# Gated cross attention on one core: how the column maxima reach all partitions, and where the gate work stands

## The reference

```
memory_proj    = memory @ W_mem.T
scores         = x @ memory_proj.T / sqrt(512)
attn           = softmax(scores)              # over the 1601 memory rows
memory_context = attn @ memory_proj
gate           = sigmoid([x, memory_context] @ W_gate.T + b_gate)
fused          = x + gate * memory_context
out            = fused * rsqrt(mean(fused**2) + 1e-6) * norm_w
```

## Time and profile before

| | us |
|---|---|
| median of three runs | 546.85 (546.77 to 548.07) |
| the profiled execution's own time | 546.85 |
| its span, first to last instruction | 544.8 |
| PE busy | 536.1 |
| DVE busy | 479.8 |
| ACT busy | 316.3 |
| POOL busy | 148.5 |

### The profile page before, as it was taken

The page is one execution under the profiler, slowest core; times in us unless marked ns, Lnnn a source line. Parts: engine busy times, 40 slices in busy tenths (PEclk is TensorE's granted clock), DMA queues, the critical chain, the costliest instruction groups (busy, mean ns, idle before and its releaser), DMA issues.

```text
span 544.8 us, 8828 instructions
## 1 busy us (share of the span) xinstructions
PE 536.1 (98%) x2432; PEld 438.8 (81%) x2432; DVE 479.8 (88%) x758; ACT 316.3 (58%) x601; POOL 148.5 (27%) x127
## 2 busy tenths in 40 slices
PE   8999999999999999999999999999999999999994
PEld 7877888888888888888888888888888888888883
DVE  3789959999799997899888997999979999789966
ACT  4676636565474755566365664666546575557523
POOL 0005600154002630046200650015400263004704
PEclk9999999999999999999999999999999999999999
DMA  9964372620575108831277114762068510301033
GB/s 227 270 130 78 93 119 67 108 72 27 137 163 113 59 0 170 176 87 39 79 132 160 62 39 111 158 106 84 12 144 165 113 49 15 120 26 40 1 117 116
DMA packets 184337, 54.25 MB, mean 100 GB/s; under 512 B 161528, under 2 KB 174848, under 8 KB 184320
## 3 DMA queue, kind: packets, MB, share of 16 engines
q1 hardware_dynamic: 183792, 53.52, 42.8%
q10 hardware_dynamic: 528, 0.52, 0.3%
HBM read 45.63 MB, written 8.39 MB: 99 GB/s over the span
## 4 chain that ended last, share of the span: by engine, by line
PE 96%; DMA 1%; DVE 1%; ACT 0%; SPq 0%; issue 0%; POOL 0%; POOLq 0%; ACTq 0%; DVEq 0%
PE bank L364 22%; PE bank L366 22%; PE bank L365 22%; PE bank L548 9%; PE bank L549 9%; PE bank L550 9%; PE bank L569 1%; PE bank L466 1%; DMA mem_raw<-in_ctx_dram 1%; PE bank L583 1%; PE bank L451 1%; PE bank L439 1%; DVE fused L1031 0%; DVE fused L1023 0%; SPq L312 0%; ACT squares_out L738 0%
## 5 line engine op out<-in xcount | busy, mean ns | idle before, releaser
L1185 POOL TENSOR_TENSOR psum_rows<-psum_rows,p_tmp 128x512 f32<-128x512 f32 (+1 forms) x88 | 123.0, 1398 | 71.6 <-ACT p_tmp L711 70.0
L875 DVE TENSOR_TENSOR p_lo<-p_tmp,p_hi 128x512 fp32r<-128x512 f32 (+1 forms) x104 | 92.6, 891 | 5.5 <-ACT p_hi L673 5.4
L1185 POOL TENSOR_TENSOR psum_rows<-p_tmp 128x512 f32<-128x512 f32 x8 | 10.4, 1300 | 276.2 <-ACT p_tmp L711 276.2
L711 ACT ACTIVATE p_tmp<-s 128x512 f32<-128x512 f32 (+1 forms) x104 | 64.5, 626 | 30.5 <-DVE s L916 29.3
L364 PE MATMUL bank<-q_hi,mt_hi 128*128 128x512 f32 (+1 forms) x208 | 81.8, 393 | 0.0
L365 PE MATMUL bank<-q_lo,mt_hi 128*128 128x512 f32 (+1 forms) x208 | 81.2, 390 | 0.0
L366 PE MATMUL bank<-q_hi,mt_lo 128*128 128x512 f32 (+1 forms) x208 | 81.2, 390 | 0.0
L548 PE MATMUL bank<-p_hi,mem_hi 128*128 128x512 f32 (+1 forms) x208 | 81.1, 390 | 0.0
L549 PE MATMUL bank<-p_lo,mem_hi 128*128 128x512 f32 (+1 forms) x208 | 81.0, 390 | 0.0
L550 PE MATMUL bank<-p_hi,mem_lo 128*128 128x512 f32 (+1 forms) x208 | 81.0, 389 | 0.0
L673 ACT ACTIVATE s<-bank 128x512 f32<-128x512 f32 (+1 forms) x104 | 62.0, 596 | 19.3 <-PE bank L366 18.9
(11 more groups left out here) (94 smaller groups left out, 1023.7 us busy)
## 6 DMA issues: line engine op xcount, KB each, us to landing
mem_raw<-in_ctx_dram SPq DMA_DIRECT2D x48, 256.0 KB, 3.0
mem_blocks<-in_ctx_dram SPq DMA_DIRECT2D x64, 136.0 KB
x_again<-in_x_dram SPq DMA_DIRECT2D x32, 256.0 KB, 2.7
out_dram<-fused SPq DMA_DIRECT2D x32, 256.0 KB, 2.1
x_raw<-in_x_dram SPq DMA_DIRECT2D x112, 64.0 KB, 2.0
mem_blocks<-in_ctx_dram SPq DMA_DIRECT2D x56, 64.0 KB, 2.0
x_raw<-in_x_dram SPq DMA_DIRECT2D x4, 256.0 KB, 4.9
gate<-in_L_xattn_W_gate_dram SPq DMA_DIRECT2D x2, 512.0 KB, 6.2
```

What stands on the lines that cost most here:

```text
L711: nc.scalar.activation(p_tmp[0:r, t % TMP_RING, :], s[0:r, t, :], ACT.Exp, scale=float(D) ** -0.5).then_inc(exp_done, 1)
L875: return nc.vector.tensor_tensor(dst, src, hi.bitcast(F32), ALU.subtract)
L1185: nc.gpsimd.tensor_tensor(psum_rows[0:r, :], a, p_tmp[0:r, t % TMP_RING, :], ALU.add).then_inc(p_added, 1)
```

## The change

The maxima of iterations 1 to 7 no longer pass through TensorE. `col_max` is written to a 2 KB DRAM tensor by one transfer and read back, broadcast to 128 partitions, by a second one into `max_rows`; both are issued by SyncE. ScalarE copies `max_rows` into MAX_BANK, with the index order mended. Iteration 0 keeps the transposes. On VectorE, gate work of tiles 1 and 2 moves ahead of the first shift; on ScalarE, tanh 2 moves ahead, and tanh 3 and squares 1 each stand one tile earlier.

```diff
+        max_out, max_in, max_spread = sem("max_out"), sem("max_in"), sem("max_spread")
-        ADD_AT = [1, 11, 12]
+        ADD_AT = [11, 12]
+        max_dram = nc.dram_tensor("max_dram", [N], F32)
     # SyncE, behind load_mem_blocks(b + 1, 1), ahead of x_again 2 and 3
+                sp.wait_ge(col_max_done, b + 1)
+                sp.dma_start(max_dram.ap().rearrange("(p j) -> p j", j=NT), col_max[:, :]).then_inc(max_out, 16)
+                sp.wait_ge(max_out, 16 * b)
+                sp.dma_start(max_rows[:, :], max_dram.ap().partition_broadcast(P)).then_inc(max_in, 16)
     # TensorE, iterations 1 to 7
                     gate_context(b - 1, 1)
-                    spread_max(b, first)
                     context(b - 1, 1)
     # ScalarE
+            def copy_max(b):
+                act.wait_ge(max_in, 16 * b)
+                act.wait_ge(r_done, b)
+                copy(bank[MAX_BANK][:, :].rearrange("q (j p) -> q j p", j=NT),
+                     max_rows[:, :].rearrange("q (p j) -> q j p", j=NT)).then_inc(max_spread, 1)
                     tanh(b - 1, 0)
                     tanh(b - 1, 1)
+                    tanh(b - 1, 2)
+                    copy_max(b)
                     for t in range(MT + 1):
...
                         softmax(b, t, first)
-                        if t in (2, 3):
-                            tanh(b - 1, t)
+                        if t == 2:
+                            tanh(b - 1, 3)
                         if t == 1:
                             squares(b - 1, 0)
-                        if t == ADD_AT[0] + 2:
+                        if t == 2:
                             squares(b - 1, 1)
     # VectorE
             def reduce_max(b, first):
                 if not first:
-                    dve.wait_ge(pe_max_rows, b)
+                    dve.wait_ge(pe_max_rows, 1)
-            def shift(b, t):
-                if t == 0:
-                    dve.wait_ge(pe_max_rows, b + 1)
+            def shift(b, t, first):
+                if t == 0 and first:
+                    dve.wait_ge(pe_max_rows, 1)
+                elif t == 0:
+                    dve.wait_ge(max_spread, b)
                     add_x(b - 1, 0)
-                    shift(b, 0)
-                    shift(b, 1)
-                    shift(b, 2)
+                    gate_ctx(b - 1, 1)
+                    gate_input(b - 1, 2)
+                    add_x(b - 1, 1)
+                    gate_ctx(b - 1, 2)
+                    shift(b, 0, first)
+                    shift(b, 1, first)
+                    shift(b, 2, first)
                     for t in range(MT):
-                        if t in (1, 2):
-                            gate_input(b - 1, t + 1)
+                        if t == 1:
+                            gate_input(b - 1, 3)
...
-                        if t in (0, 2, 4):
-                            gate_ctx(b - 1, 1 + t // 2)
+                        if t == 3:
+                            gate_ctx(b - 1, 3)
                         if t in ADD_AT:
-                            add_x(b - 1, ADD_AT.index(t) + 1)
+                            add_x(b - 1, ADD_AT.index(t) + 2)
```

More of the change, by code:

```diff
@@ L113, in xattn_kernel @@
         ident = sb("ident", [P, P])
+        max_rows = sb("max_rows", [P, N])
         ones = sb("ones", [P, 1])
@@ L441, in transpose_max, with spread_max @@
                 last.then_inc(pe_max_t, 1)
-            def spread_max(b, first):
+            def spread_max(b):
                 pe.wait_ge(col_max_done, b + 1)
-                if not first:
-                    pe.wait_ge(r_done, b)
                 for j in range(NT):
@@ L596, in iteration @@
                     weights(V[0])
-                    spread_max(b, first)
+                    spread_max(b)
                     weights(V[1])
@@ L926, in p_lo_part, with softmax @@
                 lo_part(p_lo[0:r, t % LO_RING, :], p_tmp[0:r, t % TMP_RING, :], p_hi[0:r, t, :]).then_inc(p_has_lo, 1)
-            def softmax(b, t, with_x):
+            def softmax(b, t, with_x, first):
                 if t + 3 < MT:
-                    shift(b, t + 3)
+                    shift(b, t + 3, first)
                 if with_x and t in X_AT:
@@ L1078, in iteration @@
                             mem_lo_part(b, q)
-                        softmax(b, t, not last)
+                        softmax(b, t, not last, first)
                         if t == 1:
```

## The result

| | before | after |
|---|---|---|
| median, us (the four runs of each that are compared) | 547.27 (546.77 to 548.07) | 570.62 (569.58 to 570.76) |
| profiled execution's own time | 546.85 | 569.58 |
| its span | 544.8 | 567.6 |
| mean granted clock | 0.998 | 0.986 |

The changed kernel takes 1.0411 times as long (95% interval 1.0397 to 1.0425). The direction is as forecast, the size is not: 23 us more where 5.6 were forecast, and outside of the range.

A forecast was written before the change was run, and what follows sets the result against it. TensorE was taken to bound the kernel, 96% of the chain. Stalls of 4.2 us in iterations 2 to 6, +1.9 in iteration 1 and -0.45 in iteration 7 sum to +5.6 on 546.85: 552.4 us, range 543.5 to 558.

The forecast's parts named there:

- What leaves TensorE: On TensorE, dropping the four transposes gains 0.45 us in each of iterations 1 to 7, 3.1 us in all.
- What the new path takes: From reduction through SyncE's two transfers and ScalarE's copy: the first shift starts at 236.9 instead of 233.0, bounds 236.5 and 239.
- D: Distance from the start of the reduction to the first shift on VectorE, forecast as 7.16 us.
- the issue on SyncE: First transfer issued at about 231.6, once SyncE is done with L259: 1.86 us behind the start of the reduction.
- The write: The first transfer, maxima to memory: landing taken as 1.8 us, bounds 1.5 and 4; 1.9 to the read's issue.
- The read and the copy: Second transfer, like `x_again`, median 2.7 us, then ScalarE's copy, some 0.6: 3.4 from read issued to shift.
- What the shorter lead costs: On VectorE, ScalarE and GpSimd, the new order and p_lo waiting out GpSimd's additions add 1.4 us before p_lo(9) ends.
- The deadlines: TensorE's tile 9 needs p_lo(9), slack 1.86 us, taken as tightest; without the transposes tile 9 could start at 261.4.
- S: Start of the first shift on VectorE in iteration 3: forecast 236.9, against 233.0 before, bounds 236.5 and 239.
- The tail stays: Iteration 0 and the tail behind the last iteration were forecast unchanged.
- Rival (c): The transfers decide: late write or slow broadcast reads of one row, first shift at 239, 567 us; chance 0.13.
- the sign for (c): ScalarE's copy idle for 4 us and more would show that the transfers decide.

The follow-up runs named there:

- e16: The changed kernel with SyncE's two transfers issued ahead of the memory-block loads, an unstrided copy with strided shifts, and squares 1 back behind tile 3: 546.83 us.
- e1: The changed kernel without transfers and copy, the maxima spread by TensorE's four transposes again, gate work still ahead of the shifts: 554.05 us.
- e9: e1 with squares 1 on ScalarE back in its old place behind tile 3: 549.10 us.
- e13: e1 with VectorE's split of u ahead of the four outputs of batch 6 in iteration 7: 553.72 us.
- e5: The changed kernel with bias sums 0 and 1 both at tile 2 of VectorE's list instead of tiles 3 and 4: 567.12 us.
- e15: The changed kernel with SyncE issuing both transfers of the maxima ahead of the nine memory-block loads for the next batch: 556.35 us.
- e3: The changed kernel with the second transfer reading 128 different rows of x, the maxima left out of the computation: 563.14 us.
- e11: The changed kernel with the second transfer reading one row of x, which nothing writes, 128 times, the maxima left out: 568.31 us.
- e4: The changed kernel with ScalarE's copy left unstrided and the shifts reading MAX_BANK with the stride: 569.06 us.
- e17: e16 with four copies of the maxima in memory, partition q reading copy q mod 4: 549.03 us.
- e10: The changed kernel with ScalarE issuing the transfers, unstrided copy, squares 1 back behind tile 3, and p_lo ahead of xt_lo on VectorE: 565.94 us.
- e18: e10 without its swap of p_lo and xt_lo on VectorE: 553.66 us.

## Why the prediction was wrong

Step by step, as the prediction had them.

- **What leaves TensorE: right.** The four transposes of `col_max` stand only once after, in iteration 0 (L456, four matmuls instead of 32), and where nothing waits (e16) four of six iterations are 0.4 to 0.5 us shorter.
- **What the new path takes: this step failed.** The forecast had 7.16 us in D; measured are 8.86 to 11.16, 9.82 in the mean of iterations 1 to 6. By its terms: the issue on SyncE, 1.86 forecast (2.93 in iteration 1), 2.08 measured in iterations 2 to 6 and 3.46 in the first. The reading of the trace was right, for in iterations 2 to 6 of the kernel before SyncE is done with the blocks 1.65 to 1.75 behind the start of the reduction; after, it is 1.8 to 2.5, and in e1, e9 and e13, which have the new order without the transfers, 1.8 to 2.7. So the loads of blocks stand later against the reduction once the order is changed; why is open. The write, 1.9 to the read's issue, 2.15 measured. The read and the copy, 3.4 forecast, 5.36 measured: 4.2 instead of 2.7 for a read of one place, taken over from `x_again`, whose rows are all different, and 1.07 instead of 0.6 for the copy. Over six iterations D is 14.9 us longer than forecast, and 11.8 of them are the read and the copy.
- **What the shorter lead costs: right in kind, 0.5 too much.** p_lo(9) ends 25.28 behind the shift, 25.8 forecast, so it adds 0.9 and not 1.4; the gap before p_lo(2), 0.56 us released by p_hi, and p_lo's 1.45 us beside an addition are there. That takes 3.1 us off.
- **The deadlines: one was missing.** Tile 0 waits for bias sum 1, which ends 258.40 + 0.68 - 247.05 = 12.03 behind the shift. With S at 236.9 that is 248.9, and tile 0 could start at 249.62 - 0.45 = 249.17: no wait in the forecast's own case, but only 0.2 to spare. The wait there doesn't add to the one at tile 9, it takes its place, at an earlier spot. What comes on top is the lowered clock behind it in four iterations, some 1.8 of the rest of 3.2 us. The other 1.4, 0.2 in each iteration, stand at full clock in e5 and e15 too; part of them may be the slow start behind a wait (the first matmul 0.50 us instead of 0.39), which isn't shown.
- **The tail stays: wrong.** There is a new wait for u_lo, 1.6 us, at full clock here (1.00 from 549 to 555): the span grew by 22.8 us, of which the six lengths hold 408.3 - 6 × 64.54 = 21.1, so 1.7 outside of them, where -0.45 was forecast: 2.2 more.

These are 14.9 - 3.1 + 3.2 + 2.2 = 17.2 us, as many as lie between forecast (+5.6) and the spans (+22.8). Rival (c) is what happened, for its second reason, the reads of one row, and for one that it didn't name: in iterations 1, 4 and 5 SyncE was held up 0.3 to 0.7 us longer than forecast. It had S at 239 and 567 us; S was 229.74 + 9.82 = 239.6 in the mean. Its argument against, that `x_again` never took over 3.2, was the same analogy, and its chance of 0.13 rested on it.

Of the signs named in advance, p_lo stood as releaser at tile 9 only twice, with 0.7 us, and once more elsewhere for less; shift(0) stood 8.2 behind the end of the reduction instead of 6.5, VectorE idle 2.1 instead of 0.5 us before it, and ScalarE's copy waited 15.9 us in six iterations, 4.0 in the longest: the sign for (c), which reached the 4 us that I had put on it only there.

## What to carry to other kernels

A detour through memory is two latencies in a row, and both depend on what is queued ahead on the issuing engine and on what the transfer reads: take its price from a transfer of the same shape, and if the trace has none, widen the range by what the nearest one differs in. Where a chain is made later, list every semaphore of the bounding engine that it feeds, with its slack, before the sum; the tightest one sets most of the time, the others where the wait stands; and an early wait isn't quite free, for the granted clock can fall behind it (1.8 us here). And put a latency-bound transfer ahead of bulk loads on its queue: here that place alone was worth 14 us, more than the transposes removed could ever give back.

## What the runs showed that I had not expected

- 128 reads of one 2 KB row of memory land in 3.6 to 4.7 us (in other executions of the same line 3.5 to 5.1), 128 different rows of the same size in 2.5 to 2.8 (e3), and one row that nothing wrote in 3.3 to 4.4 (e11).
- ScalarE's copy of 512 columns takes 1.07 us with a source stride of 16 bytes in SBUF and 0.60 without; VectorE's strided read from PSUM takes 0.67 either way (e4).
- A 2 KB write in pieces of 16 bytes lands in 1.4 to 2.0 us ahead of the block loads (e15, e16) and in 1.8 to 2.5 behind them, 1.4 in iteration 7, which has none; four times the pieces take 2.2 to 2.6 (e17).
- The place of one ScalarE instruction, squares 1, costs 0.5 us in each iteration (e1 against e9), and p_lo ahead of xt_lo 12 us in all (e10 against e18).
